# A two-layer attention kernel: the second attention's products, side pieces and the last gate's steps in another order

## The chip, the cores and the metric

The kernel runs on one core of one Trainium2 chip. The metric is device time in microseconds for one launch, as the median of several runs; the profile shows one execution.

## The reference

The input x is 4 batches of 1024 rows of 128 numbers. Two layers follow one another. Each normalizes x, computes an attention branch s of 16 heads of 8 and a gate branch g, and sets x = x + s * silu(g).

- First layer: full softmax attention with a layer norm and a residual of its own. Its gate is a squared-relu network whose output y drives five steps of a spiking unit: `mem = 0.9 * mem + y - reset`, with a spike where mem exceeds 1; the gate is the mean of the spikes.
- Second layer: causal softmax attention with a bias per head that is linear in the key's position. Its gate is a coupling network applied in three cycles.

## The kernel before, in words

All of x stays in on-chip memory. Four stages follow one another on the five engines' queues: a prologue (to about 55 us), the first attention (to about 533 us), the middle, which computes the coupling network (to about 600 us), and the second attention (600 to 880 us) with a short tail. The order on each engine is written out by hand, and semaphores tie the engines together.

**The second attention** (`second_attention`, line 1818) goes through 4 batches of 36 steps; the plan of a batch is made by `causal_steps` (line 1767). A step t handles 4 heads, a block of 512 queries and 128 keys, or two smaller pieces that together fill 512 columns (the diagonal blocks). For each step:

- TensorE computes the score (`score`, line 2041; the matmuls at line 2065): four matmuls of 32 rows, one per head, into two of three score slots. In steps 0, 1, 2, 9, 10 and 11 of a batch small corner matmuls (line 2056) are added to cap masked scores; steps 1, 2, 10 and 11 have two pieces and more of these.
- ScalarE takes exp of the score in two units of two heads each (line 1912), into a ring of four buffers. A score waits until the exps have freed its slots (`SLOTS = 3` units): step t may start when the first unit of step t - 1 has been read.
- POOL masks diagonal blocks (line 1937).
- TensorE multiplies the exps with the values (`product`, line 2084; matmuls at line 2104), adding into one output bank. A group of steps (0 to 4, 5 to 17, 18 to 22, 23 to 35) opens and closes the bank; VectorE then transposes it out (`lift`, line 1968, at line 1971), and the product that opens the next group waits for that.

The loop of TensorE (the last lines of `pe_part`) goes by pairs of steps, 18 a batch. In pair p it issues score 2p, the second share of product 2p - 3, the side pieces of this pair, score 2p + 1, all of product 2p - 2 and the first share of product 2p - 1. `shares` (line 2072) says how an odd step's product is split: in halves of 256 columns, or into its two pieces; one that opens a group is whole in the second share.

The **side pieces** (`second_fills`, line 1799; `piece_of`, line 2110) are other products that go through one further bank: "z" transposes the coupling network's result back (four transposes per half batch), "mix" is the output projection of the attention (32 matmuls through line 112), and "v", in batch 0, computes values of the last batch. Each is one piece in the first phase of one pair, and VectorE evacuates it (`evacuate`, line 1987). After the z of a half, ScalarE does a tanh (line 1919, in the steps of `TANH_AT`), VectorE the gate (`gate`, in the pairs of `GATE_AT`), and POOL updates x (`update`, line 1922; for the first half at step 32); SP then stores the result.

**The end of the first attention** (`first_attention`, line 899) has the same pattern, in 32 pairs a batch. VectorE's queue (`dve_part`, line 1057) goes in each pair through: the end of an output bank, the evacuations of that pair, and `extra` (line 1104), which issues the spiking unit's steps (`spike_op`, line 1073) and the steps of a row normalization (`half_norm_op`, line 830). A gate takes 18 steps: k = 0 to 12 are the spikes (`SPIKE_OPS` = 13), and k = 13 to 17 evaluate a polynomial in the spike count (lines 1088 and 1090). The second half's polynomial is put off to the next batch, but in the last batch it runs at once: k = 13 in pair 29, 14 and 15 in pair 30, 16 and 17 in pair 31. In the same pairs TensorE issues the pieces "q", "k", "v" (evacuated at line 1183) and, in the next pair, "norm" (line 1260), and each piece waits until the one before has been evacuated.

Of the kernel before, what the change touches and what calls it, by code (L numbers as in the profile page):

```python
# [25 lines left out]
B, T, C = 4, 1024, 128  # L26
# [4 lines left out]
HALF = 512  # L31
HT = HALF // P
# [113 lines left out]
CUT = HALF // 2  # L146
# [661 lines left out]
SPIKE_OPS = 1 + 3 * (STEPS - 1)  # L808
# [90 lines left out]
def first_attention(nc, a, s, ctx, room):  # L899
# [157 lines left out]
    def dve_part(dve):  # L1057
# [46 lines left out]
        def extra(b, r):  # L1104
            if b == 0 and r == 9:
                dve.wait_ge(s["wo_in"], 16 * (G + 2))
                nc.vector.tensor_scalar_mul(s["wo_x"][:, :], s["wo_x"][:, :], GATE_SCALE)
                nc.vector.tensor_scalar_mul(s["bo"][:, 0, :], s["bo"][:, 0, :], GATE_SCALE).then_inc(scaled_w, 1)
            if b == 0 and r == 13:
                dve.wait_ge(s["w1_in"], 16 * (G + 6))  # L1110
                nc.vector.tensor_scalar_mul(s["wo_x1"][:, :], s["wo_x1"][:, :], 0.5)
                nc.vector.tensor_scalar_mul(s["bo"][:, 1, :], s["bo"][:, 1, :], 0.5)
                nc.vector.tensor_scalar_mul(s["w1"][:, 0, :], s["w1"][:, 0, :], SCALE)
                nc.vector.tensor_scalar_mul(s["b_col1"][:, 0:1], s["b_col1"][:, 0:1], SCALE).then_inc(scaled_w, 1)
            if 0 < b < B and r in (2, 3):
                for k in range(SPIKE_OPS, GATED_OPS):
                    if r == (2 if k < SPIKE_OPS + 2 else 3):
                        spike_op(b - 1, 1, k)
            if b == 1 and r == 5:
                room["constants"](dve)  # L1120
            if b < B:
                if 1 <= r <= HT:
                    for n in (BT * b + 2 * r - 2, BT * b + 2 * r - 1):
                        ins = nc.vector.tensor_scalar(s["xn"][:, n, :], s["x"][:, n, :], s["mean"][:, n:n + 1],
                                                      s["skip_r"][:, n:n + 1], ALU.subtract, ALU.mult)
                    if r % 2 == 0:
                        ins.then_inc(xs0_rdy, 1)
                for k in range(GATED_OPS):
                    for hf, at in ((0, 14), (1, 23)):
                        if r == at + k // 2 and not (hf == 1 and k >= SPIKE_OPS and b < B - 1):  # L1130
                            spike_op(b, hf, k)
            for hf, at, own in ((1, 6, b - 1), (0, 29, b)):
                if 0 <= own < B and not (own == B - 1 and hf == 1):
                    first = BT * own + HT * hf
                    for k in range(HALF_NORM_OPS):
                        if r == at + k // 9:
                            if k == 0:
                                dve.wait_ge(updated, 2 * own + hf + 1)
                            half_norm_op(nc, norm1, s, work, first, k)
                    if r == at + 2:  # L1140
                        norm1.wait()
                        normed_half(nc, s, work, first, hf).then_inc(xs1_rdy, 1)
# [656 lines left out]
def second_fills(per):  # L1799

    fills = []
    for b in range(B + 1):
        def fill(kind, batch, hf, *pairs):
            fills.append((kind, batch, hf, [per // 2 * b + at for at in pairs]))

        if b == 0:
            fill("v", B - 1, 0, 2)
            fill("v", B - 1, 1, 3)
        if 0 < b < B:
            fill("mix", b - 1, 1, 4)  # L1810
        if b < B:
            fill("z", b, 0, 6)
            fill("z", b, 1, 7)
            fill("mix", b, 0, 15)
    return fills


def second_attention(nc, a, s, out_t, ctx, room):
# [5 lines left out]
    ENDS = len(closing)  # L1824
    fills = second_fills(PER1)
    LAST = S // 2 + 2
    TANH_AT = (16, 18)
    GATE_AT = (10, 11)

    def fill_index(kind, b, hf):  # L1830
        return next(n for n, one in enumerate(fills) if one[0:3] == (kind, b, hf))
# [1 line left out]
    def pieces_at(pair):  # L1833
        return [(n, kind, b, hf, pairs.index(pair), len(pairs)) for n, (kind, b, hf, pairs) in enumerate(fills)
                if pair in pairs]
# [85 lines left out]
    def pool_part(pool):  # L1921
        def update(b, hf):
            pool.wait_ge(side_in, fill_index("mix", b, hf) + 1)
            pool.wait_ge(gated, 2 * b + hf + 1)
            pool.tensor_tensor(mix[hf][:, :, :], mix[hf][:, :, :], s["y"][:, tiles(b, hf), :], ALU.mult).then_inc(scaled, 1)
            pool.wait_ge(scaled, 2 * b + hf + 1)
            x = s["x"][:, tiles(b, hf), :]
            pool.tensor_tensor(x, x, mix[hf][:, :, :], ALU.add).then_inc(updated, 1)

        def mask(t):  # L1930
            columns = plan[t % PER1][3]
            if not columns:
                return
            pool.wait_ge(expd, 2 * t + 2)
            for n in columns:
                part = probs[t % RING][:, :, n * P:(n + 1) * P]
                ins = pool.affine_select(out=part, in_=part, compare_op=ALU.is_ge, fill=0.0, base=0,  # L1937
                                         pattern=[[0, G], [1, P]], channel_multiplier=-1)
            ins.then_inc(masked, 1)

        for t in range(S):
            b, r = divmod(t, PER1)
            mask(t)
            if b > 0 and r == 14:
                update(b - 1, 1)
            if 0 < b < B - 1 and r == 5:
                pool.wait_ge(pv_done, PER1 * b)
                if b + 1 == B - 1:
                    pool.wait_ge(side_in, fill_index("v", B - 1, 1) + 1)
                spread(pool, s, b + 1).then_inc(v_rdy, 1)  # L1950
            if b == B - 1 and r == 24:
                pool.wait_ge(gated, 2 * B)
                pool.tensor_tensor(mix[1][:, :, :], s["y"][:, tiles(b, 1), :], s["bo"][:, 1:2, :].broadcast_to([P, HT, C]),
                                   ALU.mult).then_inc(lifted, 1)
                pool.wait_ge(lifted, 1)
                x = s["x"][:, tiles(b, 1), :]
                pool.tensor_tensor(x, x, mix[1][:, :, :], ALU.add).then_inc(lifted, 1)
            if r == 32:
                update(b, 0)

        pool.wait_ge(gained, 1)
        x = s["x"][:, tail_tiles(0), :]
        pool.tensor_tensor(x, x, mix[1][:, 0:2, :], ALU.add).then_inc(tailed[0], 1)
# [76 lines left out]
    def pe_part(pe):  # L2040
# [31 lines left out]
        def shares(t):  # L2072

            _, _, pieces, _, opens, _ = plan[t % PER1]
            if t % 2 == 0:
                return pieces, []
            if opens:
                return [], pieces
            if len(pieces) == 2:
                return pieces[:1], pieces[1:]  # L2080
            gs, kt, _, _, _ = pieces[0]
            return [(gs, kt, 0, 0, CUT)], [(gs, kt, CUT, CUT, HALF - CUT)]

        def product(t, share):
            b, r = divmod(t, PER1)
# [24 lines left out]
        def piece_of(n, kind, b, hf, piece, pieces):  # L2110
            if piece == 0:
                pe.wait_ge(side_in, n)
            if kind == "z":
                pe.wait_ge(twisted[b // 2], 2 * (CYCLES - 1) + b % 2 + 1)
                for t in range(HT):
                    ins = nc.tensor.transpose(side_tiles[:, t, :], s["y"][:, BT * b + HT * hf + t, :], s["ident"][:, :])
            elif kind == "v":
                pe.wait_ge(*room["freed"][1])
                for t in range(HT):
                    ins = by_columns(nc, side_tiles[:, t, :], kept_xt[hf][:, t * P:(t + 1) * P], s["w1"][:, 2, :])  # L2120
            else:
                pe.wait_ge(on_rdy, 2 * b + hf + 1)
                for t in range(HT):
                    ins = by_columns(nc, side_tiles[:, t, :], on[hf][:, t * P:(t + 1) * P], s["wo_x1"][:, :])
            if piece == pieces - 1:
                ins.then_inc(side_ps, 1)

        for pair in range(LAST):
            if 2 * pair < S:
                score(2 * pair)  # L2130
            if pair == 2:
                product(1, 0)
            if 0 <= 2 * pair - 1 - LAG1 < S:
                product(2 * pair - 1 - LAG1, 1)
            for one in pieces_at(pair):
                piece_of(*one)
            if 2 * pair < S:
                score(2 * pair + 1)
            if 0 <= 2 * pair - LAG1 < S:
                product(2 * pair - LAG1, 0)  # L2140
                if pair > 1:
                    product(2 * pair + 1 - LAG1, 0)
        for k in range(2):
            pe.wait_ge(tail_on, k + 1)
            for t in (2 * k, 2 * k + 1):
# [112 lines left out]
```

## Time and profile before

| | us |
|---|---|
| median of 3 runs | 892.6 |
| lowest, highest | 889.99, 892.78 |
| the profiled execution | 890.42 |
| its span, first to last instruction | 888.7 |
| ScalarE busy | 828.0 (93%) |
| TensorE busy | 783.5 (88%) |
| VectorE busy | 420.5 (47%) |
| POOL busy | 217.9 (25%) |

The profile names TensorE PE, its weight loads PEld, VectorE DVE, ScalarE ACT, and a number such as L1912 is a line of the kernel. Busy times are shares of the whole span and mean little for one stage; the rows further down are of single stretches. A matmul's recorded time overlaps with the next one's, so the time from one start to the next is what counts for TensorE.

### The profile page before, as it was taken

Reading aid. Unit: us, or ns where it says so; the run is one execution under the profiler, and the core shown is the slowest. Engines: PE = TensorE matmul, PEld = TensorE weight load, DVE = VectorE, ACT = ScalarE, POOL = GpSimd, SP = SyncE. Lnnn points to the kernel's source line nnn. Section 1 sums busy time; section 2 is a strip of 40 time slices with the busy share of each in tenths; the row PEclk is TensorE's granted clock in tenths of the full one; section 3 lists DMA queues with packets and bytes.
Section 4 is the critical chain, followed back from the end, with each engine's and each line's share of the span. In section 5 each row is a group of like instructions: output and inputs, shape, how many; then the busy total and the mean of one; then the engine's idle time right before and its main releaser. Section 6 shows DMA issues by size and latency. Waiting matters only on the chain.

```text
span 888.7 us, 22278 instructions
## 1 busy us (share of the span) xinstructions
PE 783.5 (88%) x9422; PEld 306.7 (35%) x9422; DVE 420.5 (47%) x894; ACT 828.0 (93%) x921; POOL 217.9 (25%) x260
## 2 busy tenths in 40 slices
PE   4949999899999999999999999988888888888876
PEld 2412434234343433433343333223333332333322
DVE  7821174464657653677428588995111121121122
ACT  7759999999999999999999995779999999999996
POOL 2201120121212041111302023104343344334343
PEclk9969999999999999999999999997999999999999
DMA  6882020110210301103000016000202202022000
GB/s 186 283 287 46 2 77 2 34 45 2 77 49 1 125 2 34 69 25 124 1 3 25 26 58 208 24 25 2 76 2 89 59 31 89 24 66 89 13 1 25
DMA packets 31949, 53.46 MB, mean 60 GB/s; under 512 B 5480, under 2 KB 16360, under 8 KB 31848
## 3 DMA queue, kind: packets, MB, share of 16 engines
q1 hardware_dynamic: 31848, 52.01, 18.5%
q8 instruction: 76, 1.25, 0.6%
q14 instruction: 25, 0.20, 0.1%
HBM read 31.29 MB, written 20.71 MB: 59 GB/s over the span
## 4 chain that ended last, share of the span: by engine, by line
PE 70%; ACT 17%; DVE 4%; issue 3%; ACTq 0%; DVEq 0%
PE c_ps L1225 26%; PE c_ps L1210 13%; ACT c_ring L1912 11%; PE c_ps L112 10%; PE c_ps L2104 10%; PE c_ps L2065 7%; ACT c_ring L1011 4%; PE c_ps L1632 1%; DVE early L1577 1%; PE c_ps L1647 1%; PE c_ps L1639 1%; ACT xs L1919 1%; ACT c_ring L1435 1%; DVE y L1580 1%; ACT c_th L1456 0%
## 5 line engine op out<-in xcount | busy, mean ns | idle before, releaser
L1011 ACT ACTIVATE c_ring<-c_ps 128x1024 f32<-128x1024 f32 x512 | 473.4, 1033 | 11.0 <-PE c_ps L1210 10.7
L1912 ACT ACTIVATE c_ring<-c_ps 128x1024 f32<-128x1024 f32 x288 | 268.9, 1051 | 7.5 <-PE c_ps L2065 6.2
L1225 PE MATMUL c_ps<-c_ring,vt 128*18 128x256 f32 (+1 forms) x3072 | 271.7, 456 | 0.0
L1210 PE MATMUL c_ps<-q_st,k_st 32*128 32x512 f32 x1024 | 130.8, 499 | 27.2 <-ACT c_ring L1011 20.8
L2104 PE MATMUL c_ps<-c_ring,vt 128*18 128x256 f32 (+3 forms) x1856 | 153.0, 438 | 1.2 <-DVE ext L1971 0.2
L1937 POOL TENSOR_SCALAR_AFFINE_SELECT c_ring<-c_ring 128x512 f32<-128x512 f32 x128 | 86.6, 696 | 187.3 <-ACT c_ring L1912 187.3
L2065 PE MATMUL c_ps<-q_st,k_st 32*128 32x512 f32 (+3 forms) x768 | 80.0, 419 | 45.9 <-ACT c_ring L1912 45.2
L1225 PEld LDWEIGHTS c_ps<-c_ring,vt 128*18 128x18 f32 x3072 | 64.9, 97 | 143.1 <-issue 103.8
L1210 PEld LDWEIGHTS c_ps<-q_st,k_st 32*128 32x128 f32 x1024 | 50.4, 183 | 142.8 <-ACT c_ring L1011 133.5
L1032 POOL TENSOR_TENSOR early<-early 128x512 f32<-128x512 f32 x32 | 38.4, 1200 | 177.2 <-DVE early L1149 177.2
L2065 PEld LDWEIGHTS c_ps<-q_st,k_st 32*128 32x128 f32 x768 | 39.0, 186 | 108.2 <-ACT c_ring L1912 95.2
L1971 DVE STREAM_TRANSPOSE ext<-c_ps 128x512 f32<-128x512 f32 x15 | 10.8, 717 | 133.9 <-PE c_ps L2104 133.9
L2104 PEld LDWEIGHTS c_ps<-c_ring,vt 128*18 128x18 f32 x1856 | 40.7, 97 | 69.8 <-issue 51.6
L1149 DVE TENSOR_SCALAR early<-c_ps 128x512 f32<-128x512 f32 x32 | 22.1, 690 | 63.6 <-PE c_ps L112 63.6
L1153 DVE TENSOR_SCALAR y<-c_ps,rho 128x128 f32<-128x128 f32 x32 | 9.0, 344 | 83.4 <-PE c_ps L112 83.4
L1018 POOL TENSOR_TENSOR early<-early,y 128x512 f32<-128x512 f32 x7 | 10.6, 1511 | 142.7 <-DVE early L1164 142.7
L1435 ACT ACTIVATE c_ring<-c_ps,cn_b 128x512 f32<-128x512 f32 (+1 forms) x30 | 25.1, 858 | 16.8 <-PE c_ps L1632 9.6
L1040 POOL TENSOR_TENSOR c_th<-parts 128x512 bf16<-128x512 f32 x12 | 15.4, 1287 | 82.7 <-DVE parts L1181 82.7
L112 PE MATMUL c_ps<-proj_t,early 128*32 128x128 f32 x1024 | 33.8, 273 | 0.0
L112 PE MATMUL c_ps<-y,fc_t 128*32 128x512 f32 x256 | 33.3, 592 | 0.0
L112 PEld LDWEIGHTS c_ps<-proj_t,early 128*32 128x32 f32 x1024 | 29.3, 110 | 5.9
L1097 DVE SCALAR_TENSOR_TENSOR c_th<-ext,c_th 128x512 f32<-128x512 f32 x24 | 25.4, 1060 | 0.7
(241 smaller groups left out, 746.2 us busy)
## 6 DMA issues: line engine op xcount, KB each, us to landing
q_st<-q_hl SPq DMA_DIRECT2D x48, 256.0 KB
k_st<-k_hl SPq DMA_DIRECT2D x48, 256.0 KB
q_hl<-parts SPq DMA_DIRECT2D x12, 512.0 KB, 4.3
k_hl<-parts SPq DMA_DIRECT2D x12, 512.0 KB, 4.5
q_hl<-early SPq DMA_DIRECT2D x4, 512.0 KB, 4.8
k_hl<-early SPq DMA_DIRECT2D x4, 512.0 KB, 5.3
out_dram<-x SPq DMA_DIRECT2D x7, 256.0 KB, 3.9
x<-in_L_attn_x_dram SPq DMA_DIRECT2D x3, 512.0 KB, 5.4
```

Source lines behind the costliest of these rows:

```text
L112: ins = nc.tensor.matmul(out[c:c + COLUMN, :], weight[:, c:c + COLUMN], rows, start=start, stop=stop, tile_position=(0, c))
L1011: nc.scalar.activation(probs[t % RING][:, 2 * pair:2 * pair + 2, :], scores[unit % SLOTS][:, :, :], ACT.Exp).then_inc(expd, 1)
L1032: pool.tensor_tensor(hidden[f], hidden[f], hidden[f], ALU.mult).then_inc(hid_rdy, 1)
L1097: ins = nc.vector.scalar_tensor_tensor(y if step == STEPS - 1 else count[:, :, :], m1, 1.0, count[:, :, :], ALU.is_gt, ALU.add)
L1149: ins = nc.vector.tensor_scalar_max(hidden[hf[1]], side[:, :], 0.0)
L1210: ins = nc.tensor.matmul(scores[(2 * t + i // 2) % SLOTS][:, i % 2, :], k_st[part, g, kt * P:(kt + 1) * P], q_st[part, g, qh * HALF:(qh + ...
L1225: ins = nc.tensor.matmul(o_ps[32 * h:32 * h + 2 * W9, c0:c1], vt[b % 2][:, kt, gp, h, W9 * gs:W9 * gs + 2 * W9], probs[t % RING][:, h, c0: ...
L1435: nc.scalar.activation(out, source, ACT.Gelu, bias=bias[:, 0:1]).then_inc(squashed[z], 1)
L1912: nc.scalar.activation(probs[t % RING][:, first:first + 2, :], scores[unit % SLOTS][:, :, :], ACT.Exp).then_inc(expd, 1)
L1937: ins = pool.affine_select(out=part, in_=part, compare_op=ALU.is_ge, fill=0.0, base=0, pattern=[[0, G], [1, P]], channel_multiplier=-1)
L2065: ins = nc.tensor.matmul(banks[i][:, at:at + w], k_st[part, 2 * gp + gs, kt * P:(kt + 1) * P], q_st[part, 2 * gp + gs, qh * HALF + q0:qh * ...
L2104: ins = nc.tensor.matmul(o_ps[32 * h:32 * h + 2 * W9, q0:q0 + w], vt[b % 2][:, kt, gp, h, W9 * gs:W9 * gs + 2 * W9], probs[t % RING][:, h, ...
```

## The change

In the second attention each phase gets one whole product: an odd step's product goes whole into the second share, that is behind the next even score, unless the pair it belongs to has a side piece. There it is split into a quarter and three quarters (or its two pieces, the second first). Side pieces are spread over two pairs, half of their tiles in each; the v pieces of batch 0 move from pairs 2 and 3 to pairs 10 to 13, z from 6 and 7 to 6 to 9, mix gets a second pair. The tanhs go from steps 16 and 18 to 17 and 21, the second gate from pair 11 to 12, POOL's update from step 32 to 34. In the first attention's last batch step k = 15 goes to pair 31, and 16 and 17 to the pair after the batch.

```diff
+                        if r == at + k // 2 and not (hf == 1 and k > SPIKE_OPS):
+                            if hf == 0 or k < SPIKE_OPS or b == B - 1:
+                                spike_op(b, hf, k)
+                if b == B - 1 and r > 29:
+                    spike_op(b, 1, SPIKE_OPS + r - 29)
+            if b == B and r == 0:
+                for k in range(SPIKE_OPS + 3, GATED_OPS):
+                    spike_op(b - 1, 1, k)
...
+        if 0 < b < B:
+            fill("mix", b - 1, 1, 4, 5)
+        if b < B:
+            fill("z", b, 0, 6, 7)
+            fill("z", b, 1, 8, 9)
         if b == 0:
-            fill("v", B - 1, 0, 2)
-            fill("v", B - 1, 1, 3)
-        if 0 < b < B:
-            fill("mix", b - 1, 1, 4)
+            fill("v", B - 1, 0, 10, 11)
+            fill("v", B - 1, 1, 12, 13)
         if b < B:
-            fill("z", b, 0, 6)
-            fill("z", b, 1, 7)
-            fill("mix", b, 0, 15)
+            fill("mix", b, 0, 15, 16)
...
-    TANH_AT = (16, 18)
-    GATE_AT = (10, 11)
+    TANH_AT = (17, 21)
+    GATE_AT = (10, 12)
+    QUARTER = HALF // 4
...
-            if r == 32:
+            if r == 34:
                 update(b, 0)
...
-            if opens:
+            if opens or not pieces_at((t + 3) // 2):
                 return [], pieces
             if len(pieces) == 2:
-                return pieces[:1], pieces[1:]
+                return pieces[1:], pieces[:1]
             gs, kt, _, _, _ = pieces[0]
-            return [(gs, kt, 0, 0, CUT)], [(gs, kt, CUT, CUT, HALF - CUT)]
+            return [(gs, kt, 0, 0, QUARTER)], [(gs, kt, QUARTER, QUARTER, HALF - QUARTER)]
...
+            own = range(HT // pieces * piece, HT // pieces * (piece + 1))
             if kind == "z":
...
-                for t in range(HT):
+                for t in own:
...
-            if pair == 2:
-                product(1, 0)
...
-                product(2 * pair - LAG1, 0)
-                if pair > 1:
-                    product(2 * pair + 1 - LAG1, 0)
+                product(even - LAG1, 0)
+                product(odd - LAG1, 0)
```

## Rows read from the trace of the kernel before

**Rows 1.** The page's costliest groups: busy, mean ns of one | idle before, releaser.
```profile
L1912 ACT ACTIVATE c_ring<-c_ps 128x1024 f32<-128x1024 f32 x288 | 268.9, 1051 | 7.5 <-PE c_ps L2065 6.2
```

**Rows 2.** ScalarE's timeline, second attention: start, us, what, [idle before, releaser].
```profile
600.73 8.00 ACT L1912 ACTIVATE c_ring<-c_ps 128x1024 f32<-128x1024 f32 x8
...
612.29 13.10 ACT L1912 ACTIVATE c_ring<-c_ps 128x1024 f32<-128x1024 f32 x14 [0.94 <-PE c_ps L2065]
...
635.02 0.63 ACT L1919 ACTIVATE xs<-y 128x512 f32<-128x512 f32 x1
...
675.40 3.77 ACT L1912 ACTIVATE c_ring<-c_ps 128x1024 f32<-128x1024 f32 x4 [0.39 <-PE c_ps L2065]
...
689.20 5.77 ACT L1912 ACTIVATE c_ring<-c_ps 128x1024 f32<-128x1024 f32 x6 [0.44 <-PE c_ps L2065]
...
848.52 31.66 ACT L1912 ACTIVATE c_ring<-c_ps 128x1024 f32<-128x1024 f32 x34
```

**Rows 3.** ScalarE's timeline, a short stretch from 646 us.
```profile
646.30 4.68 ACT L1912 ACTIVATE c_ring<-c_ps 128x1024 f32<-128x1024 f32 x5
```

**Rows 4.** Busy time by stretch: window, length, busy (count) by engine, PEclk, DMA.
```profile
600.00:611.00 11.00, 8.12 (x67) 3.76 (x71) 8.57 (x7) 10.06 (x11) 7.28 (x6) 0.53 0.01 2
611.00:880.00 269.00, 225.51 (x2892) 89.89 (x2888) 46.54 (x77) 262.45 (x287) 101.90 (x142) 1.00 0.15 46
```

**Rows 5.** TensorE's timeline, a plain odd phase.
```profile
646.55 0.51 PE L2065 MATMUL c_ps<-q_st,k_st 32*128 32x512 f32 x4 [0.92 <-ACT c_ring L1912]
646.99 1.49 PE L2104 MATMUL c_ps<-c_ring,vt 128*18 128x256 f32 x24
648.41 0.51 PE L2065 MATMUL c_ps<-q_st,k_st 32*128 32x512 f32 x4
```

**Rows 6.** TensorE's timeline, scores of steps 1 to 4 of batch 1.
```profile
672.40 0.50 PE L2065 MATMUL c_ps<-q_st,k_st 32*128 32x384 f32 x6 [0.60 <-ACT c_ring L1912]
...
673.38 1.49 PE L2104 MATMUL c_ps<-c_ring,vt 128*18 128x512 f32 x16
674.80 0.50 PE L2065 MATMUL c_ps<-q_st,k_st 32*128 32x256 f32 x6
...
675.69 0.63 PE L2104 MATMUL c_ps<-c_ring,vt 128*18 128x256 f32 x8
676.57 0.51 PE L2065 MATMUL c_ps<-q_st,k_st 32*128 32x512 f32 x4 [0.25 <-ACT c_ring L1912]
677.25 1.70 PE L2104 MATMUL c_ps<-c_ring,vt 128*18 128x512 f32 x16 [0.17 <-DVE ext L1971]
678.88 0.51 PE L2065 MATMUL c_ps<-q_st,k_st 32*128 32x384 f32 x8
```

**Rows 7.** TensorE's timeline, step 8 of batch 1 with a mix piece.
```profile
686.15 0.51 PE L2065 MATMUL c_ps<-q_st,k_st 32*128 32x512 f32 x4 [0.34 <-ACT c_ring L1912]
686.74 1.05 PE L2104 MATMUL c_ps<-c_ring,vt 128*18 128x512 f32 x8
687.59 1.07 PE L112 MATMUL c_ps<-wo_x,on 128*32 128x128 f32 x32
688.60 0.51 PE L2065 MATMUL c_ps<-q_st,k_st 32*128 32x512 f32 x4
```

**Rows 8.** POOL's timeline, the first attention's last pairs.
```profile
527.67 1.42 POOL L1040 TENSOR_TENSOR c_th<-parts 128x512 bf16<-128x512 f32 x1 [3.86 <-DVE parts L1181]
```

**Rows 9.** VectorE's timeline, the same pairs.
```profile
527.51 2.13 DVE L1090 SCALAR_TENSOR_TENSOR ext<-ext,y 128x512 f32<-128x512 f32 x2
...
531.01 0.68 DVE L1183 TENSOR_TENSOR xn<-c_ps,bv 128x512 f32<-128x512 f32 x1
...
535.97 0.72 DVE L1066 STREAM_TRANSPOSE early<-c_ps 128x512 f32<-128x512 f32 x1 [1.33 <-PE c_ps L1225]
```

**Rows 10.** TensorE's timeline, the same pairs.
```profile
531.75 0.39 PE L1260 MATMUL c_ps<-c_th,head_of 128*32 128x512 bf16 x2 [0.73 <-DVE xn L1183]
```

**Rows 11.** TensorE's timeline, a whole product at the low clock.
```profile
606.68 1.91 PE L2104 MATMUL c_ps<-c_ring,vt 128*18 128x512 f32 x8
```

More of the change, by code:

```diff
@@ L1129, in extra @@
                     for hf, at in ((0, 14), (1, 23)):
-                        if r == at + k // 2 and not (hf == 1 and k >= SPIKE_OPS and b < B - 1):
-                            spike_op(b, hf, k)
+                        if r == at + k // 2 and not (hf == 1 and k > SPIKE_OPS):
[6 more added lines that the diff above has]
+                    spike_op(b - 1, 1, k)
             for hf, at, own in ((1, 6, b - 1), (0, 29, b)):
@@ L2118, in piece_of @@
                 pe.wait_ge(*room["freed"][1])
-                for t in range(HT):
+                for t in own:
                     ins = by_columns(nc, side_tiles[:, t, :], kept_xt[hf][:, t * P:(t + 1) * P], s["w1"][:, 2, :])
@@ L2122, in piece_of @@
                 pe.wait_ge(on_rdy, 2 * b + hf + 1)
-                for t in range(HT):
+                for t in own:
                     ins = by_columns(nc, side_tiles[:, t, :], on[hf][:, t * P:(t + 1) * P], s["wo_x1"][:, :])
@@ L2128, in pe_part @@
         for pair in range(LAST):
-            if 2 * pair < S:
-                score(2 * pair)
-            if pair == 2:
-                product(1, 0)
-            if 0 <= 2 * pair - 1 - LAG1 < S:
-                product(2 * pair - 1 - LAG1, 1)
+            even, odd = 2 * pair, 2 * pair + 1
+            if even < S:
+                score(even)
+            if 0 <= even - 1 - LAG1 < S:
+                product(even - 1 - LAG1, 1)
             for one in pieces_at(pair):
                 piece_of(*one)
-            if 2 * pair < S:
-                score(2 * pair + 1)
-            if 0 <= 2 * pair - LAG1 < S:
-                product(2 * pair - LAG1, 0)
-                if pair > 1:
-                    product(2 * pair + 1 - LAG1, 0)
+            if even < S:
+                score(odd)
+            if 0 <= even - LAG1 < S:
+                product(even - LAG1, 0)
+                product(odd - LAG1, 0)
         for k in range(2):
```

## The prediction

> **What bounds the kernel now.** I read the page first, then ScalarE's timeline from 600 us on, where the second attention runs, then the table of clocks by stretch, then TensorE's timeline against ScalarE's, and last VectorE's around 530 us.
>
> The page gives the 288 exps of the second attention 268.9 us of busy time and 7.5 us of idle time before them, 6.2 of it put down to the score products [rows 1]. The exps run from 600.73 to 848.52 + 31.66 = 880.18 us [rows 2], and what follows is a tail of 8.5 us. So the stage takes 279.45 us on ScalarE. Five exps that nothing holds take 4.68 us [rows 3]: with the last one's 1.05 us [rows 1] taken off, four intervals of 0.905. At that pace 288 exps take 260.6, and the eight tanhs at most 0.63 each [rows 2], 5.0: 13.8 us of the stage are waits, more than the page calls idle, since back-to-back exps overlap by 0.14 and a short delay shows no idle.
>
> TensorE is what they wait for. I call a phase the time from one step's score to the next step's score. A step has two exps, so ScalarE asks for a score every 1.81 us. A score may start once the first exp of the step before has ended, 1.05 after that exp's start, and an exp follows its score's start by 0.60 (674.80 to 675.40, 688.60 to 689.20) [rows 2, 6, 7]: 1.65 of the 1.81 are gone before any signalling, so the score arrives just in time at best. No reserve is carried from one phase to the next; **a phase costs ScalarE whatever it has over 1.81**, and what it has under is lost to nobody. The clock is at the full level of 2.4 GHz from 611 us on and at 1.2 GHz for most of 600 to 611 (mean 0.53 of full) [rows 4].
>
> Now the prices. A plain score takes 0.44 (646.55 to 646.99), one and a half products with the switch back to a score 1.42 (to 648.41) [rows 5]. A whole product takes 0.85 (686.74 to 687.59), a full mix piece 1.01 (to 688.60) [rows 7]. So a half product is 0.43, three quarters 0.64, a quarter 0.21, the switch 0.14. The scores of steps 1 and 2, with corner products, take 0.98 (672.40 to 673.38) and 0.89 (674.80 to 675.69) [rows 6]; steps 10 and 11 are built alike, so they take the same.
>
> Before, the odd phases (score plus one and a half products) are 1.86 when plain, and too long wherever something is added: step 1 has 0.98 + 1.42 = 2.40, step 3 has 2.31 (676.57 to 678.88) [rows 6], step 11 has 0.89 + 1.42 = 2.31, and steps 15, 21 and 33, whose pieces make one and three quarter products, 0.44 + 1.63 = 2.07. Step 8 has the whole mix piece, 2.45 [rows 7]; step 9, with one corner product (about 0.14), I put at 0.44 + 0.14 + 1.42 = 2.0. Over 1.81 these are 0.59, 0.50, 0.50, 3 x 0.26, 0.64 and 0.2: **3.2 us a batch**. ScalarE's idle times of 0.39 behind step 1 and 0.44 behind step 8 [rows 2] are the same waits less the 0.14 of overlap.
>
> **The change, part by part.** *Products.* Without a side piece each phase now has one score and one whole product: 0.44 + 0.85 + 0.14 = 1.43, with 0.38 to spare. With side pieces the first phase has three quarters and half a piece, 0.44 + 0.64 + 0.50 + 0.14 = 1.72, the second a whole and a quarter, 1.64. All these are under 1.81. Left over in batches 1 to 3:
> - step 1: 0.98 + 0.85 + 0.14 = 1.97, over by 0.16;
> - step 2: 0.89 + 0.85 + 0.14 = 1.88, over by 0.07. The product that closes an output bank now runs whole in this phase and ends later, and the next product waits for VectorE's transpose out of that bank. From 675.69 to 677.25 a half product and this wait took 1.56 [rows 6], so the wait is 1.13. Now 0.89 + 0.85 + 1.13 = 2.87 after step 2's score, 0.99 into step 3's phase; with 0.85 + 0.14 that phase has 1.98, over by 0.17;
> - step 8: 2.45 less half a mix piece, 1.95, over by 0.14;
> - step 10: 0.98 + 0.64 + 0.50 = 2.12, over by 0.31; step 11: 0.89 + 0.85 + 0.21 + 0.14 = 2.09, over by 0.28; step 13 (a second share of half a product) 1.86, over by 0.05.
>
> Together 1.18 where 3.2 was: 2.0 a batch, **6.0** in three. In batch 0 the opening is slow: 612.29 - 600.73 = 11.56 for ten exps where 9.05 would do [rows 2]. Most of that is the low clock and stays; the v piece that stood ahead of the score at 612.29 goes to pair 10, and with it I take 0.85 of the 0.94 idle shown there. The rest of batch 0 falls from 0.2 + 0.50 + 0.78 to 0.16 + 0.28 + 0.05: 1.0. **Sum here 7.9.** Bounds: nothing gained, if the waits only move, and 13.8 less the 1.6 that stay at the start, 12.2. I take the phase sums, as their rows are of the very instructions.
>
> *What I cost at nothing.* The tanhs of steps 17 and 21 need the z evacuated; its second half is issued in phase 14 (18), over 5 us (2.5) earlier, and were that cover gone ScalarE itself would stand. The gates and POOL's update two steps later hide behind VectorE and POOL, mostly idle here; the update's output store is one DMA on SP, queued between loads that wait for half a batch each. POOL's mask for step 36 stands behind that update and would delay its product if the update's two operations ran past step 35. The v rows are read first in batch 2. The tail keeps its products and its length.
>
> *Polynomial steps.* In the first attention's last pairs TensorE waits 0.73 us at 531.75 for the v evacuation [rows 10], queued on VectorE behind two polynomial steps [rows 9]. One of the two goes behind it, the last two behind the next evacuation as well. The pair took 2.13, of which one step is 0.7 and the other 1.4; POOL's squares ran from 527.67 for 1.42 beside them [rows 8]. The second step looks held by POOL, so the small operation that moves into its place would be held until about 529.1 instead: the evacuation comes 0.6 sooner. If the step is long by itself, 1.4 sooner, cut to 0.73 by the wait that there is. Bounds 0 and 0.73; I take **0.6**. The moved steps end before the 1.33 that VectorE waits at 535.97 [rows 9] is used up: 0.7 earlier start, 0.7 more work.
> The Trainium skill (SBUF — State Buffer, "Who interferes with whom") has VectorE instructions with two SBUF inputs and POOL's reads exclude one another for a whole instruction. By that rule the next operation, which has two such inputs, inherits the hold and the gain is the 0.6; without it the cut 0.73. The trace agrees with it as far as a 1.4 us step beside POOL's 1.42 goes.
>
> **Sum.** 7.9 + 0.6 = 8.5 off the profiled execution's 890.42 (span 888.7 and 1.7 around it): 881.9. That execution lies 2.2 below the median 892.6 of three runs (889.99 to 892.78), and I can't tell which of them the changed kernel's median goes with; I add half, 1.0: **882.9 us**.
>
> **Rivals.** *ScalarE nearer to its floor.* The last 34 exps took 31.66 with no idle shown [rows 2], 0.928 each. If that is the floor and not 0.905, a phase may have 1.86; the waits before are 279.45 - 267.2 - 5.0 = 7.2, those left 0.83 a later batch and 1.9 in batch 0, 4.4. Gain 2.8 + 0.6, time 888. Against: rows 3. Chance 0.08.
> The Trainium skill (ScalarE: Activation LUTs, "What ACT_TABLE_LOAD costs") gives 186 ns plus 0.833 per element less about 93 of overlap, by estimate 0.946 per exp, and 889. The trace agrees in the length, 1.05, and differs in the overlap, 0.14.
>
> *The waits only move.* Phases with a half side piece have but 0.09 to spare. Were each of the 34 (four fills of two in batches 1 to 3, five in batch 0) 0.3 longer through the added switches between score, product and piece, they would lose 0.21 each, 7.1 in all, and the time would be 881.9 + 7.1 + 1.0 = 890. For it: the switch is known in one order only. Chance 0.08.
>
> *A slower clock.* TensorE now pauses before every score instead of long before every second. If the clock fell in the second attention, a whole product's 1.05 would become the 1.91 of the start [rows 11], a phase 1.43 x 1.8 = 2.6, 0.8 over. The low stretch at the start was about 10.3 us [rows 4], four phases: 3.1 lost each. From the fourth such stretch the kernel is slower by over 0.3%: 881.9 + 12.4 + 1.0 = 895. Against: the pauses get shorter (0.92 to 0.38) and the clock held through the long ones. Chance 0.05.
>
> **How the numbers follow.** The forecast has 0.79. 0.3%, about what a measurement of this kernel can tell from no change, is 2.7 us, so faster means under 889.9. Faster: 0.79 + 0.08 and, of the slow clock, nothing: 0.87. Same: 0.08. Slower: 0.05. Range: downwards the sum without the added 1.0 and with half of the 4.3 that part the 7.9 from its bound, 879.7, rounded to 879. Upwards the first rival with a little room: 888.5.
>
> **What would show it.** Right: ScalarE's idle before the exps falls from 6.2 us to about 2, what is left standing at steps 2, 4, 11 and 12; a plain pair of TensorE shows two pauses of about 0.4; exps from first to last take about 271.5 us; the wait at 531.75 is gone or 0.1. Wrong: phases with half pieces over 1.81, exps 0.928 apart where TensorE is early, or the clock under 1 after 611 us.

## The result and the profile after

The changed kernel takes 883.48 us, the median of five runs (883.34 to 886.11), where the kernel before took 892.6 (five runs, 889.99 to 892.93). The ratio estimated from all these runs is 0.9919, 95% interval [0.9905, 0.9933]; the two medians alone are 9.1 us apart, a ratio of 0.990. Runs of one kernel spread over 2 to 3 us, so I compare the profiled executions, 890.42 and 883.34: 7.1 us less. A later comparison of the two on one chip gave 884.13 and 891.71, 7.6 us and 0.9923 [0.9909, 0.9937].

The page of the kernel after, its span and the second attention's exps (busy, mean ns of one | idle before, releaser):

```profile
span 881.6 us, 21910 instructions
...
L1920 ACT ACTIVATE c_ring<-c_ps 128x1024 f32<-128x1024 f32 x288 | 268.0, 1069 | 2.7 <-PE c_ps L2073 2.3
```

The idle time put down to the score products fell from 6.2 us [rows 1] to 2.3. ScalarE's timeline shows where:

```profile
599.76 7.99 ACT L1920 ACTIVATE c_ring<-c_ps 128x1024 f32<-128x1024 f32 x8
608.45 1.94 ACT L1920 ACTIVATE c_ring<-c_ps 128x1024 f32<-128x1024 f32 x2 [0.70 <-PE c_ps L2073]
610.72 13.00 ACT L1920 ACTIVATE c_ring<-c_ps 128x1024 f32<-128x1024 f32 x14 [0.34 <-PE c_ps L2073]
...
643.16 46.48 ACT L1920 ACTIVATE c_ring<-c_ps 128x1024 f32<-128x1024 f32 x50
689.85 1.94 ACT L1920 ACTIVATE c_ring<-c_ps 128x1024 f32<-128x1024 f32 x2 [0.22 <-PE c_ps L2073]
691.95 11.11 ACT L1920 ACTIVATE c_ring<-c_ps 128x1024 f32<-128x1024 f32 x12 [0.16 <-PE c_ps L2073]
...
847.27 25.85 ACT L1920 ACTIVATE c_ring<-c_ps 128x1024 f32<-128x1024 f32 x28
```

The exps run from 599.76 to 847.27 + 25.85 = 873.12: 273.36 us for the stage where 279.45 were [rows 2], 6.1 less. In a batch two pauses are left that show as idle time, 0.22 and 0.16, in front of the exps of steps 11 and 12, that is behind the phases of steps 10 and 11. TensorE's timeline, from a plain pair through the long steps of batch 1 (the number behind x counts matmuls):

```profile
664.67 0.50 PE L2073 MATMUL c_ps<-q_st,k_st 32*128 32x512 f32 x4 [0.35 <-ACT c_ring L1920]
665.10 1.06 PE L2112 MATMUL c_ps<-c_ring,vt 128*18 128x384 f32 x16
666.50 0.50 PE L2073 MATMUL c_ps<-q_st,k_st 32*128 32x512 f32 x4 [0.35 <-ACT c_ring L1920]
...
670.17 0.50 PE L2073 MATMUL c_ps<-q_st,k_st 32*128 32x384 f32 x6 [0.19 <-ACT c_ring L1920]
...
672.14 0.50 PE L2073 MATMUL c_ps<-q_st,k_st 32*128 32x256 f32 x6
...
674.01 0.51 PE L2073 MATMUL c_ps<-q_st,k_st 32*128 32x512 f32 x4
675.01 1.05 PE L2112 MATMUL c_ps<-c_ring,vt 128*18 128x512 f32 x8 [0.49 <-DVE ext L1979]
676.00 0.51 PE L2073 MATMUL c_ps<-q_st,k_st 32*128 32x384 f32 x8
...
683.26 0.51 PE L2073 MATMUL c_ps<-q_st,k_st 32*128 32x512 f32 x4 [0.34 <-ACT c_ring L1920]
683.85 1.05 PE L2112 MATMUL c_ps<-c_ring,vt 128*18 128x512 f32 x8
684.71 0.63 PE L112 MATMUL c_ps<-wo_x,on 128*32 128x128 f32 x16
685.27 0.51 PE L2073 MATMUL c_ps<-q_st,k_st 32*128 32x512 f32 x4
...
687.06 0.50 PE L2073 MATMUL c_ps<-q_st,k_st 32*128 32x384 f32 x6
...
689.25 0.50 PE L2073 MATMUL c_ps<-q_st,k_st 32*128 32x256 f32 x6
...
691.35 0.50 PE L2073 MATMUL c_ps<-q_st,k_st 32*128 32x512 f32 x4
```

One pause of 0.92 and none before the next score [rows 5] has become two of 0.35. The phases are read from score to score: step 1 is 672.14 - 670.17 = 1.97, step 2 1.87, step 3 1.99, step 8 2.01, step 10 2.19, step 11 2.10. The clock, by the table of stretches:

```profile
600.00:611.00 11.00, 9.09 (x67) 3.87 (x71) 7.60 (x7) 9.73 (x11) 7.82 (x7) 0.54 0.00 0
611.00:873.00 262.00, 228.09 (x2712) 85.79 (x2708) 47.33 (x77) 260.58 (x286) 99.32 (x142) 1.00 0.15 47
```

It is as before [rows 4]: low at the opening alone. And the end of the first attention, VectorE's, POOL's and TensorE's rows in the timeline:

```profile
527.16 0.68 DVE L1090 SCALAR_TENSOR_TENSOR ext<-ext,y 128x512 f32<-128x512 f32 x1
...
527.32 1.42 POOL L1040 TENSOR_TENSOR c_th<-parts 128x512 bf16<-128x512 f32 x1 [3.85 <-DVE parts L1187]
527.76 1.00 DVE L263 TENSOR_TENSOR a_fix<-a_fix,a_var 128x4 f32<-128x4 f32 x1
...
529.18 0.16 DVE L263 TENSOR_TENSOR a_fix<-a_fix,a_var 128x4 f32<-128x4 f32 x1
...
530.04 0.68 DVE L1189 TENSOR_TENSOR xn<-c_ps,bv 128x512 f32<-128x512 f32 x1
...
530.78 0.40 PE L1266 MATMUL c_ps<-c_th,head_of 128*32 128x512 bf16 x2
```

The norm's matmul no longer waits; it starts at 530.78 against 531.75 [rows 10]. Of these 0.97, 0.34 are older than the moved steps: the score that stands at 526.19 in the trace before stands at 525.85 here. One polynomial step stands ahead of the evacuation, at its plain 0.68, and the small operation behind it took 1.00 us instead of 0.16, beside POOL's 1.42.

**How I read the waits.** My count of waits by the starts of the exps turned out to be a bad measure. The same timeline in narrower windows gives the first exps of two of the runs above, one behind a pause and one in the last stretch, by themselves:

```profile
691.95 1.02 ACT L1920 ACTIVATE c_ring<-c_ps 128x1024 f32<-128x1024 f32 x1 [0.16 <-PE c_ps L2073]
...
847.27 1.10 ACT L1920 ACTIVATE c_ring<-c_ps 128x1024 f32<-128x1024 f32 x1
```

With the first one's length taken off, the ends of the twelve exps lie (11.11 - 1.02) / 11 = 0.917 apart, those of the last 28 (25.85 - 1.10) / 27 = 0.917. The starts behind a pause are closer, mostly 0.904, and the recorded length grows from 1.02 to 1.10 within some eight exps. So ScalarE completes an exp every **0.917 us**, two in 1.83, and in a long run a start up to 0.08 late costs nothing. Counted by ends, what 288 exps have over that pace (and over 0.52 for a tanh, the time from its start to the next exp's) is 11.3 us before and 5.2 after: the whole 6.1. By batch it is 3.5, 2.6, 2.7, 2.5 before and 2.2, 0.9, 1.1, 0.9 after (the third batch has 0.2 more in front of step 29 in both, where the score had come in time; why is open). Where I say what a step costs, it is the excess of the exps behind that step's phase. The experiments below are counted so, each from its one profiled execution.

### The profile page after: what moved, and what is told of

Its sections match the earlier page's. It is cut to its first block, busy times and chain, and to the rows that moved or that the text cites. A ratio compares the mean times of both kernels' runs of the same rounds, so it can differ in the third digit from the quotient of the medians.

```text
span 881.6 us, 21910 instructions
## 1 busy us (share of the span) xinstructions
PE 786.7 (89%) x9238; PEld 302.3 (34%) x9238; DVE 421.4 (48%) x894; ACT 826.6 (94%) x921; POOL 215.9 (24%) x260
## 4 chain that ended last, share of the span: by engine, by line
PE 69%; ACT 18%; DVE 4%; issue 3%; DVEq 0%; ACTq 0%
PE c_ps L1231 26%; PE c_ps L1216 13%; ACT c_ring L1920 12%; PE c_ps L112 10%; PE c_ps L2073 8%; PE c_ps L2112 8%; ACT c_ring L1011 4%; PE c_ps L1638 1%; DVE early L1583 1%; PE c_ps L1653 1%; ACT xs L1927 1%; PE c_ps L1645 1%; ACT c_ring L1441 1%; DVE y L1586 1%; ACT c_th L1462 0%
## 5 line engine op out<-in xcount | busy, mean ns | idle before, releaser
L2112 PE MATMUL c_ps<-c_ring,vt 128*18 128x384 f32 (+3 forms) x1672 | 153.2, 468 | 2.3 <-issue 0.9
L1945 POOL TENSOR_SCALAR_AFFINE_SELECT c_ring<-c_ring 128x512 f32<-128x512 f32 x128 | 84.4, 678 | 182.6 <-ACT c_ring L1920 182.5
L1231 PEld LDWEIGHTS c_ps<-c_ring,vt 128*18 128x18 f32 x3072 | 64.9, 97 | 143.1 <-issue 103.8
L1979 DVE STREAM_TRANSPOSE ext<-c_ps 128x512 f32<-128x512 f32 x15 | 10.8, 717 | 93.9 <-PE c_ps L2112 93.9
L2112 PEld LDWEIGHTS c_ps<-c_ring,vt 128*18 128x18 f32 x1672 | 35.4, 97 | 58.9 <-issue 44.0
L2000 DVE COPY y<-c_ps 128x512 f32<-128x512 f32 x8 | 5.5, 692 | 57.9 <-PE c_ps L2125 57.9
```

What stands on the lines that cost most here:

```text
L1231: ins = nc.tensor.matmul(o_ps[32 * h:32 * h + 2 * W9, c0:c1], vt[b % 2][:, kt, gp, h, W9 * gs:W9 * gs + 2 * W9], probs[t % RING][:, h, c0: ...
L2112: ins = nc.tensor.matmul(o_ps[32 * h:32 * h + 2 * W9, q0:q0 + w], vt[b % 2][:, kt, gp, h, W9 * gs:W9 * gs + 2 * W9], probs[t % RING][:, h, ...
```

## The experiments

Time is the median; ratios are to the kernel before, run on the same chip. Differences from the changed kernel are to its 883.48, measured apart from them: the kernel before had medians of 891.0 to 892.6 in such groups of runs, so a difference of about 1 us is read from the traces.

**The polynomial steps alone.** The kernel before, with the new conditions of the polynomial steps and nothing else:

```
-  if r == at + k // 2 and not (hf == 1 and k >= SPIKE_OPS and b < B - 1):
-      spike_op(b, hf, k)
+  if r == at + k // 2 and not (hf == 1 and k > SPIKE_OPS):
+      if hf == 0 or k < SPIKE_OPS or b == B - 1:
+          spike_op(b, hf, k)
...
```

> The kernel before with the move of the polynomial steps alone. My theory: TensorE's 0.73 us wait for the v evacuation near 531 us shrinks to about 0.1, the small normalization step that moves into the held place takes about 1.0 instead of 0.16 beside POOL's squares, and the first exp of the second attention starts 0.6 us earlier measured from the last exp of the first attention's steady stretch; total 0.6 us below the kernel before, which timing alone can hardly tell from nothing. Rival (the moved work only reappears at the end of the bank or in the middle): first exp as late as before, 0.0. The second attention stays at 279.4 us from first exp to end of the last.

890.21 us (ten runs, 889.38 to 892.49) against 891.01 (19 runs): 0.9993 [0.9982, 1.0005]. A gain of this size is inside the spread, so I read it in the trace, from a score in front to the norm's matmul behind, which takes out where the execution happened to stand:

```profile
526.48 0.50 PE L1216 MATMUL c_ps<-q_st,k_st 32*128 32x512 f32 x4
...
531.42 0.39 PE L1266 MATMUL c_ps<-c_th,head_of 128*32 128x512 bf16 x2
```

That is 4.94 with the steps moved. With them in the old place (the next experiment) it is 5.55:

```profile
526.79 0.50 PE L1210 MATMUL c_ps<-q_st,k_st 32*128 32x512 f32 x4
...
532.34 0.39 PE L1260 MATMUL c_ps<-c_th,head_of 128*32 128x512 bf16 x2 [0.73 <-DVE xn L1183]
```

The 0.61 lasts: from the same score to the first exp of the second attention it is 600.40 - 526.48 = 73.92 here and 601.32 - 526.79 = 74.53 there. The second attention itself took 279.93 in this execution, 0.5 more than I expected, all of it at one pause of the opening:

```profile
612.46 13.10 ACT L1918 ACTIVATE c_ring<-c_ps 128x1024 f32<-128x1024 f32 x14 [1.43 <-PE c_ps L2071]
```

The order of work there is that of the kernel before, which had 0.94 at this place [rows 2]. What differs is how long the clock stayed low behind the first exp. The table of stretches for the kernel before, this one, the changed kernel and a second execution of the changed kernel:

```profile
610.00:615.00 5.00, 5.00 (x112) 2.86 (x107) 0.69 (x1) 4.07 (x5) 1.70 (x3) 0.95 0.01 3
610.00:615.00 5.00, 5.00 (x100) 3.04 (x96) 0.69 (x1) 3.57 (x5) 1.38 (x3) 0.88 0.01 3
610.00:615.00 5.00, 4.39 (x56) 1.50 (x52) 0.00 (x0) 4.67 (x6) 1.22 (x2) 0.99 0.01 3
610.00:615.00 5.00, 4.38 (x52) 1.49 (x48) 0.00 (x0) 4.43 (x6) 1.26 (x3) 0.88 0.01 3
```

A mean of 0.95 is half a microsecond at half the clock, so the clock is full from 610.5, 611.2, 610.1 and 611.2 on: 9.8, 10.8, 10.3 and 10.9 us behind the first exp (600.73, 600.40, 599.76, 600.29). The step in question cost 1.04, 1.54, 0.44 and 0.68 by ends.

**The products and pieces alone.** The changed kernel with the old conditions of the polynomial steps (the diff above, reversed).

> The changed kernel with the polynomial steps back in their old place. My theory: second attention from first exp to end of the last exp 273.4 us as in the changed kernel, total 0.6 us above the changed kernel and 6.1 to 6.5 below the kernel before. Rival (the parts interact, for instance by shifting the low-clock stretch at the start of the second attention): the stage differs by more than 0.5 us from 273.4.

885.08 us (884.88 to 885.31), 0.9935 [0.9917, 0.9953]. The exps take 273.46 us, as in the changed kernel (273.36), and have 5.3 over the pace for its 5.2. So the second attention's gain is of the products and pieces alone, and in the traces the two parts add up. The medians tell less: 5.9 below the kernel before (6.1 to 6.5 expected) and 1.6 above the changed kernel (0.6 expected).

**Side pieces whole.** One fill, one pair, as before the change; the products stay new:

```
-  fill("mix", b - 1, 1, 4, 5)
+  fill("mix", b - 1, 1, 4)
-  fill("z", b, 0, 6, 7)
+  fill("z", b, 0, 6)
...
```

> The changed kernel with each side piece whole in the first pair of its two. My theory, by phases: a first phase with a whole mix or v piece has 0.44 + 0.64 + 1.01 = 2.09, with a whole z 2.0, so 0.28 and 0.17 over 1.81, step 8 with the mix piece 2.45; step 10 loses its half piece and gets 1.97. Per later batch 0.85 us more waits, 1.1 in batch 0: stage and total 3.6 us above the changed kernel (2.5 to 4). Rival (halving only adds switches and hides nothing): no difference within 0.5 us.

885.25 us (885.04 to 885.89), 0.9939 [0.9920, 0.9957]: 1.8 us over the changed kernel, half of what I expected. Only 1.0 of it is in the exps, 274.35 us for 273.36; the first exp came 0.4 later, ahead of anything that the edit touches, and the tail took 0.5 longer, with the clock at 0.50 for its last matmuls and 1.00 in the changed kernel. ScalarE's pause behind step 8 is back at its old size [rows 2], and the one behind step 10 is gone:

```profile
643.19 42.90 ACT L1920 ACTIVATE c_ring<-c_ps 128x1024 f32<-128x1024 f32 x46
686.54 5.67 ACT L1920 ACTIVATE c_ring<-c_ps 128x1024 f32<-128x1024 f32 x6 [0.45 <-PE c_ps L2073]
```

By ends step 8 costs 0.55 (0.11 with halves), step 10 0.07 (0.31), the other mix piece at step 30 0.18, and in batch 0 each whole v piece and the mix piece 0.18. The whole z pieces cost nothing. Batch 0 has 2.0 over the pace all the same, for 2.2: in its opening, where the two kernels are alike, the clock was full 8.6 us behind the first exp and the step of 0.44 cost nothing. So halving is worth 0.4 a later batch, and half of what it saves at step 8 is lost again at step 10, whose corner products leave no room for the second half. I had priced whole pieces at 0.85 a batch.

**Odd products in halves always.** The products as before the change (first half of the next odd product in the even one's phase), the pieces in halves:

```
-  if opens or not pieces_at((t + 3) // 2):
+  if opens:
-  return pieces[1:], pieces[:1]
+  return pieces[:1], pieces[1:]
-  return [(gs, kt, 0, 0, QUARTER)], [(gs, kt, QUARTER, QUARTER, HALF - QUARTER)]
+  return [(gs, kt, 0, 0, CUT)], [(gs, kt, CUT, CUT, HALF - CUT)]
```

> The changed kernel with odd products split in the old way, in halves or first piece first, in every pair; side pieces stay in halves. My theory: odd phases have one and a half products again, so steps 1, 3, 9, 11, 15, 21 and 33 are over by 0.59, 0.50, 0.2, 0.50 and three times 0.26, and most of the gain is lost: 5 to 6.5 us above the changed kernel. Rival (spreading the side pieces is what helps): at most 2 us above the changed kernel.

888.95 us (ten runs, 888.37 to 892.06), 0.9982 [0.9970, 0.9993]: 5.5 over the changed kernel, and most of the gain is gone. The profiled execution took 891.25, 2.3 above that median, and its exps take 6.4 us longer than the changed kernel's. The waits over the pace by batch are 5.1, 2.1, 2.3, 2.1, with steps 1, 3 and 11 at 0.50, 0.4 and 0.47, as in the kernel before. Of the 6.4, 3.6 are of the later batches. The rest is the opening, where this kernel takes the first odd product early (a pair earlier than the kernel before), in front of the scores, at the low clock, which lasts longer as well, with a mean of 0.59 from 611 to 616 us:

```profile
610.70 4.00 ACT L1920 ACTIVATE c_ring<-c_ps 128x1024 f32<-128x1024 f32 x4 [1.98 <-PE c_ps L2073]
615.82 11.21 ACT L1920 ACTIVATE c_ring<-c_ps 128x1024 f32<-128x1024 f32 x12 [1.12 <-PE c_ps L2073]
```

```profile
611.00:616.00 5.00, 4.30 (x44) 1.51 (x40) 0.00 (x0) 3.76 (x5) 1.23 (x2) 0.59 0.02 3
```

Whether the early product keeps the clock low or another execution would have had it back sooner is open. The later batches are at the full clock, and there the whole product per score is the part that carries the change: 1.2 of the 1.6 us that a batch gained, and the halved pieces (above) the other 0.4.

**The v pieces early.** In halves at pairs 2 to 5 of batch 0 instead of 10 to 13:

```
+  if b == 0:
+      fill("v", B - 1, 0, 2, 3)
+      fill("v", B - 1, 1, 4, 5)
...
```

> The changed kernel with the v pieces of batch 0 in halves at pairs 2 to 5, ahead of z, instead of 10 to 13. My theory: the slow opening of the second attention gets half a v piece back before the score of step 5, so the wait at that step grows from 0.45 to about 0.95 us, steps 8 and 10 to 11 of batch 0 get half pieces and 0.1 to 0.3 us each: 0.8 to 1.0 us above the changed kernel. Rival (the place of the v pieces is indifferent): no difference in batch 0 within 0.2 us.

885.92 us (884.1 to 886.47); the profiled execution, 884.10, is 0.8 above the changed kernel's. Batch 0 has 2.8 over the pace for 2.2. It is a small loss, as expected, and not much more than two executions of one kernel differ by (the changed kernel's wait behind step 4 was 0.44 in one execution and 0.68 in another). The steps behind it did as expected: 0.11 at step 8, 0.31 and 0.26 at steps 10 and 11 (0, 0.06 and 0.26 in the changed kernel).

**Products of a quarter.** Every product of the second attention is cut to 128 columns; the rest of the sum is left out. It was to show ScalarE's pace with TensorE early everywhere.

```
+  w = min(w, P)
```

> The changed kernel with every product cut to at most 128 of its columns; the other columns of the attention's sum are left out. No phase is near 1.81 us, so ScalarE alone sets the pace. First exp to end of the last: 266 to 267 us if 0.905 per exp is the floor (my forecast's value), 272 to 273 if 0.928 is (first rival). The changed kernel's trace, where exps in a row grow by 0.013 each in length while they start 0.905 apart, speaks for 0.917 and 269.8.

905.89 us in the one run that there is, slower than all others with far less work. The exps took 294.8 us, outside all three forecasts. The table of stretches and TensorE's timeline tell why:

```profile
600.00:680.00 80.00, 63.46 (x751) 32.97 (x751) 19.11 (x26) 76.27 (x82) 28.62 (x37) 0.62 0.15 43
...
800.00:880.00 80.00, 62.99 (x724) 31.40 (x728) 13.71 (x24) 74.60 (x79) 28.04 (x38) 0.59 0.09 29
```

```profile
702.81 0.51 PE L2073 MATMUL c_ps<-q_st,k_st 32*128 32x512 f32 x4 [0.61 <-ACT c_ring L1920]
...
706.47 0.80 PE L2073 MATMUL c_ps<-q_st,k_st 32*128 32x512 f32 x4
...
708.53 0.80 PE L2073 MATMUL c_ps<-q_st,k_st 32*128 32x512 f32 x4 [0.27 <-ACT c_ring L1920]
```

The granted clock fell to the 1.2 GHz level again and again, mean 0.6 for most of the stage. A score then takes 0.80 for 0.51, and since the next score waits for an exp that waits for this one, the phase grows to 708.53 - 706.47 = 2.06, although TensorE pauses in it. What I wanted is readable only where the clock was nearly full, as in this run of ScalarE (two windows that share an exp: the second of the pair is the first of the eleven), with the table's row for the stretch:

```profile
696.08 2.00 ACT L1920 ACTIVATE c_ring<-c_ps 128x1024 f32<-128x1024 f32 x2
...
696.99 10.25 ACT L1920 ACTIVATE c_ring<-c_ps 128x1024 f32<-128x1024 f32 x11
```

```profile
696.00:706.00 10.00, 7.16 (x113) 3.79 (x112) 0.92 (x2) 10.00 (x12) 6.82 (x9) 0.95 0.01 2
```

The pair ends at 698.08 and the eleventh exp at 707.24: ten steps of 0.916. That pace holds with products a quarter as long, so it is not TensorE's products that set it. This run alone leaves a rival, the hand-over itself: here each score starts 0.145 behind the end of an exp of 1.09, and the next exp 0.60 behind the score's start, which makes 1.83 for two exps too. The starts behind a pause decide it. In the kernel before, the score of 646.55 has ended at 647.06 [rows 5] and its exp starts at 647.21, 0.15 later where 0.09 is enough when the exp waits for it; exps are 1.03 long there, so the hand-over has time to spare, and their ends are still 0.916 apart. So the pace is ScalarE's own.

**Side pieces past the corner steps.** What the changed kernel still loses stands at steps 8, 10 and 11, where halves of the mix piece meet corner products. Here they go to pairs 7 and 8, everything behind them later:

```
-  fill("mix", b - 1, 1, 4, 5)
+  fill("mix", b - 1, 1, 7, 8)
-  fill("z", b, 0, 6, 7)
-  fill("z", b, 1, 8, 9)
+  fill("z", b, 0, *((9, 10) if b else (7, 8)))
+  fill("z", b, 1, *((11, 12) if b else (9, 10)))
...
-  TANH_AT = (17, 21)
-  GATE_AT = (10, 12)
+  TANH_AT = (23, 27)
+  GATE_AT = (13, 15)
...
```

> The changed kernel with the side pieces moved off steps 8 to 11, where corner products already fill TensorE: mix of the half before at pairs 7 and 8, z at 9 to 12 (7 to 10 in batch 0), v at 11 to 14, with tanhs, gates and POOL's updates behind them. My theory: the waits at steps 9, 11 and 12 of later batches fall from 0.2, 0.35 and 0.27 to 0, 0.15 and 0.07, batch 0's at step 12 likewise: 1.2 to 2 us below the changed kernel, the last exp earlier by as much and the tail unchanged. Rival (the later gates and POOL's last updates come to stand at the end): the stage shortens but the tail grows by 1 us or more.

882.75 us (882.30 to 883.36), 0.9909 [0.9892, 0.9926]; the tail behind the last exp is 8.5 us as in the changed kernel, against the rival. To tell it from the changed kernel both ran side by side:

> The changed kernel itself, without an edit, beside the next one on the same chip. Both theories: about 883.4 where its runs fall on the lower of their two levels and 885.9 on the upper one; ratio to the kernel before 0.992.

> The same later side pieces as in the first such run, now beside the changed kernel. If the three waits that went (steps 9, 11 and 12) were worth what their exps show, 0.15 to 0.3 each in three batches less the 0.08 that a stall gets back, it lies 0.7 to 1.0 below the changed kernel at the same level, 882.4 to 882.8 and 0.999 of it; if they only move to the later pairs, it lies within 0.3 of it, 883.1 to 883.7.

The changed kernel took 884.13 us (883.84 to 885.88, four of five within 0.5, so between the two times that I had put), the edited one 882.09 (881.86 to 882.50), 0.9896 [0.9881, 0.9911] of the kernel before. It lies 2.0 below the changed kernel, at the upper end of my first forecast and above the second, and no run of the one reaches a run of the other. The three waits of a later batch went from 0.7 to 0.1 together; the second forecast took 0.08 off each, which counting by ends has off already. Its page and timeline:

```profile
L1920 ACT ACTIVATE c_ring<-c_ps 128x1024 f32<-128x1024 f32 x288 | 267.3, 1070 | 1.7 <-PE c_ps L2073 1.1
```

```profile
655.04 59.15 ACT L1920 ACTIVATE c_ring<-c_ps 128x1024 f32<-128x1024 f32 x64
...
722.37 59.16 ACT L1920 ACTIVATE c_ring<-c_ps 128x1024 f32<-128x1024 f32 x64
```

64 exps stand in a row without a pause where the changed kernel had two; by ends a later batch has 0.3 to 0.5 over the pace instead of 0.9 to 1.1. Of the 3.6 us that are left, 2.4 stand in batch 0.

## Why the prediction was right, and where it was off

The forecast was 882.9; 883.48 came, inside the range and on the side I gave 0.87. The sum itself was less good than that: it put the profiled execution at 881.9, and it was 883.34. The 1.0 added for the median made up for most of the difference, and after the change the median happened to lie only 0.14 above the profiled execution. That the forecast came within 0.6 us is thus in part luck. Of the 7.1 us between the profiled executions 6.1 are the second attention's, 0.6 the polynomial steps', and the rest is time that the execution after was ahead by before the moved steps.

- **Products, 7.9 forecast, 6.1 measured.** This is the term that was mis-sized, and the step that failed is the price behind it: "a phase costs ScalarE whatever it has over 1.81", with "No reserve is carried from one phase to the next". The phases themselves came as worked out: 1.97, 1.87, 1.99, 2.01, 2.19 and 2.10 for 1.97, 1.88, 1.98, 1.95, 2.12 and 2.09. But ScalarE needs 1.83 for two exps, and a late start gets 0.08 back. I had taken the pace from the starts of five exps [rows 3], which stand right behind a late one. The rows could have told: 0.59 and 0.64 less 0.14 of overlap are 0.45 and 0.50, where ScalarE's idle times are 0.39 and 0.44 [rows 2]. By ends the waits of a later batch before were 2.6, not 3.2 (step 1 0.50 for 0.59, step 8 0.55 for 0.64, steps 15, 21 and 33 0.17 for 0.26: each 0.09 less), and those after 0.9 to 1.1, not 1.18. The eight waits of before got 0.6 a batch back between them, the seven smaller ones of after 0.25. The gain is 4.8 in three batches for 6.0: the price was too high by some 0.09 at each full wait, so the sum was most too high where the waits were many.
- **Steps after.** Steps 1, 2 and 3 cost 0.07, 0.04 and 0.11 to 0.15 for 0.16, 0.07 and 0.17, step 8 0.11 for 0.14, and steps 10 and 11 0.31 and 0.26 for 0.31 and 0.28. The last two follow step 8 closely, with no time to earn the 0.08 again. (The sum for step 10 left out the 0.14 for the switch that the plain phase with half a piece has; of it 0.07 came, 2.19 for 2.12.) The bank's transpose held the next product as worked out: 675.01 is 1.00 into step 3's phase, forecast 0.99.
- **Batch 0, 1.85 forecast, 1.3 measured.** The pause of 0.94 became 0.34: 0.60 for the 0.85 I took. How much of that difference is the two executions' is not settled, but the clock was full 9.8 us behind the first exp before and 10.3 after, and the two executions of the old order lay 0.5 apart at this step for 1.0 us of low clock. Read between them, the old order would have cost about 1.3 at 10.3 us, by estimate, and the v piece was worth about 0.85, as forecast. The other steps gave 0.66 for 1.0, by the same refund and a new 0.1 where a v half now stands.
- **Polynomial steps, 0.6 forecast, 0.61 measured**, shown alone and lasting to the first exp. The hold went where the inherited case had it: the 0.16 us operation took 1.00. The page of the Trainium skill named in the prediction (SBUF — State Buffer, "Who interferes with whom") would have it so, and this trace agrees: 1.00 ends at 528.76, with POOL's 1.42 ending at 528.74.
- **ScalarE nearer to its floor** was half right: 0.917 lies between my 0.905 and the rival's 0.928. It read the pace over 34 exps, as one should, but left the tail of small waits in it, and it had all waits pay it in full. That the pace is ScalarE's own is shown with the kernel of quarter products above.
  By the Trainium skill (ScalarE: Activation LUTs, "What ACT_TABLE_LOAD costs") my estimate had been 0.946. The traces do not bear that out: 0.917.
- **The waits only move** failed: a half mix piece takes 685.27 - 684.71 = 0.56 for the 0.50 of my sum, 0.06 more for the switch and not 0.3, and the halved z pieces cost no wait at all.
- **A slower clock** did not come, 1.00 from 611 us on. But the mechanism is real in this kernel: with products of a quarter the same loop ran at a mean of 0.6, and took 22 us longer than the changed kernel. I had against it that pauses get shorter; in that kernel they were shorter than before too, and the clock fell. The changed kernel has the work of before, only spread, and kept its clock; that this is the reason is not shown.
- **What would show it:** the idle time fell to 2.3 (forecast about 2), the plain pauses are 0.35 (about 0.4), the wait at 531.75 is gone; the stage takes 273.4 and not 271.5, which is the term above.

## What to carry to other kernels

The pace of a pipelined engine is read from the ends of a long run of its instructions, with the first one's length taken off, and never from a few starts behind a pause. Where two engines hand one tile back and forth in a short loop, work beside the loop is free up to the time between two hand-overs and costs what is above it, less the little that a late start gets back (0.08 here): so even out the phases first (3.6 of the 4.8 us of the later batches here), then halve only those pieces that don't fit, and keep them away from phases that are long already (another 2.0 in all). Small work cut away from such a loop can cost more than it saves if the clock falls with it: look at the granted clock of every experiment that leaves work out.

## What was not expected of the hardware

- Behind a pause exps of 128x1024 start 0.904 apart and are recorded as 1.02 long, growing to 1.10; completed ones lie 0.917 apart throughout. A length recorded for one such instruction (mean 1.07) is thus neither its cost nor constant.
- With products of a quarter TensorE's clock fell to the lower level for most of the stage, out of a stretch with pauses of 0.5 to 0.8 us before each score. The length of a pause alone does not tell when that happens: the kernel before had pauses of 0.92 before every second score [rows 5], with one and a half products between them, and kept 1.00.
- An operation of 128x4 that takes 0.16 us elsewhere took 1.00 beside POOL, more than six times as long. This one was forecast; at this place what VectorE's operation costs went by the end of POOL's instruction and not by its size (ends at 528.76 and 528.74 here, 529.39 and 529.37 in the kernel with the polynomial steps alone).
- How long the low clock lasts at the opening differs between executions, 8.6 to 10.9 us behind the first exp where the order of work there is the same, and one step's wait goes with it: in the new order 0 at 8.6, 0.44 at 10.3 and 0.68 at 10.9. What two executions of one kernel differ by in their exps stands at this step (0.5 us of 0.5 in the old order, 0.2 of 0.2 in the new). Why the clock comes back earlier or later was not looked into.
